# Thirteen products of the identity with itself on TensorE around the start of a decoder layer's output projection

## Chip, cores and metric

The kernel runs on one core of a Trainium2 chip. The metric is the device time of one execution in microseconds, here the median of three.

## What is computed

One pre-norm decoder layer over `x` (4 x 512 tokens, 512 wide): causal self-attention with 32 heads of width 16 in 8 key groups, cross-attention with 8 heads on `ctx_2048`, and a feed-forward part whose weights are rounded to -1, 0, 1 and whose activations are rounded to 8 bits.

```python
x = x + _L0_attn_ref(_layernorm(x), Wq, Wk, Wv, Wo)
x = x + _L0_xattn_ref(_layernorm(x), ctx_2048, ctx_2048)
x = x + _L0_ffn_ref(_layernorm(x), w_gate, w_up, w_down)

# in _L0_attn_ref
w = jax.nn.softmax(scores, axis=-1)
ctx = jnp.einsum('bgjqk,bkgd->bqgjd', w, v).reshape(b, s, D)
return ctx @ Wo.T
```

## The kernel before

The program has two blocks. Each gives every engine a list of instructions of its own; semaphores join them, and at a block's end all five engines meet (L237) before the next block begins.

**First block**, `attention`: `project_qkv` makes queries, keys and values batch by batch, and `self_attention` works in steps i. There are `COUNT` = 32 units (4 batches x 8 key groups, 4 heads each), and `LAST` = COUNT + 5 = 37, so i runs to 36. A step holds stages of several units: `first_scores` for unit i, `second_scores` for i - 2, `weigh` (probabilities by values, L870) for i - 3 and `turn_outputs` (L836) for i - 4. Each stage has its own test that the unit exists. In `turn_outputs` TensorE turns the unit's summed values (`b_osb`, copied out of PSUM by ScalarE at L797) with four transposes by the identity; VectorE then takes the reciprocal of the sums (L806) and writes the divided outputs into `tok` (L809), which holds all 16 token tiles.

**Second block**, `rest_of_layer`: `attend_output(c)` for c = 0, 1, ... works on 16 tiles of 128 tokens. On TensorE it turns tile c with four transposes (L1518), and then projects tile c - 1 with twelve matmuls of 128x512 (L1528): four slices of the contraction, each in three products of high and low parts (`hi`, `lo`, `wo_hi`, `wo_lo`). ScalarE writes the high part of the turned tile (L1211), VectorE the low part (L1354); TensorE waits for the low part ahead of the projection. VectorE then adds the rows of x (L1365, loaded by SyncE at L1023) and takes the moments (L1346, L1349), GpSimd makes the factor (L1150 to L1156), ScalarE normalises (L1217, L1222), VectorE splits (L1359), and SyncE stores the result to DRAM (L1028). SyncE's queue also carries the loads of context rows (L1010) and query rows (L1016) for the cross-attention. GpSimd begins the block with three memsets (L1129 to L1132). Cross-attention and the feed-forward part follow in `attend_context` and `feed`.

The order on each engine is that of the code. `ident` is a 128x128 identity in f32, `p2[0]` the PSUM bank `ab_j2` (in which second scores are made) and `pd` a bank that the second block first uses for the sums of cross-attention. At the kernel's start there is a function `rouse` already (L609): it multiplies ones by ones, f32 128x128, into a bank that nothing reads: 12 times at first, twice after the first batch's second tile is turned, and four times after its fourth.

Of the kernel before, what the change touches and what calls it, by code (L numbers as in the profile page):

```python
# [13 lines left out]
P = 128  # L14
# [37 lines left out]
def due(value):  # L52

    return not isinstance(value, int) or value > 0
# [21 lines left out]
class Steps:  # L76
# [3 lines left out]
    LAST = COUNT + 5  # L80
# [31 lines left out]
def bank_free(pe, st, keep, i, k):  # L112
    if st.holder(i, k) is not None:
        pe.wait_ge(keep["p1_used"], st.holder(i, k) + 1)


def first_scores(nc, pe, st, keep, i, k):

    if not i < st.COUNT:
        return  # L120
    s = i % UNROLL
    if k == 0:
        pe.wait_ge(keep["stacks_in"][s], 16 * st.STACK_LOADS * (i // UNROLL + 1))
    bank_free(pe, st, keep, i, k)
    for j, qt, c in st.units[k]:
        w = (qt + 1) * P
        last = nc.tensor.matmul(st.bank(keep, i, k)[:, c:c + w], keep["qs"][0:STACK, s, j, qt * P:(qt + 1) * P], keep["ks"][0:STACK, s, 0:w],  # L127
                                start=True, stop=True)
    last.then_inc(keep["p1_full"], 1)


def turn_maxima(nc, pe, st, keep, i):
    if 0 <= i - 1 < st.COUNT:
        pe.wait_ge(keep["p1_used"], st.use[i - 1, st.nu - 1] + 1)
        bank_free(pe, st, keep, i, st.TURN)
        nc.tensor.transpose(st.bank(keep, i, st.TURN)[0:st.BLOCKS, 0:P], keep["mx"][:, (i - 1) % 2, :], keep["ident"][:]).then_inc(keep["p1_full"], 1)
# [556 lines left out]
def self_attention(nc, ctx, io, scr, keep, st):  # L693


    STEPS, LAST = st.COUNT, st.LAST
# [11 lines left out]
    p2, pv = keep["p2"], keep["pv"]  # L708
# [16 lines left out]
    def pblock(s, kb):  # L725
        return probs[:, s, at[kb]:at[kb] + GSZ * width[kb]].rearrange("p (j w) -> p j w", j=GSZ)
# [97 lines left out]
    def tensor(pe):  # L824
        pe.wait_ge(keep["lo_done"], TILES)
        pe.wait_ge(keep["scaled"], 1)
        pe.wait_ge(keep["padded"], 2)
        for i in range(st.EARLY_STEPS, LAST):
            j2, j3, j4 = i - 2, i - 3, i - 4

            def turn_outputs():
                if 0 <= j4 < STEPS:
                    pe.wait_ge(osb_full, j4 + 1)
                    bank_free(pe, st, keep, i, OUT)
                    for t in range(TPB):
                        last = nc.tensor.transpose(st.bank(keep, i, OUT)[:, t * P:(t + 1) * P], osb[:, j4 % 2, t * P:(t + 1) * P], keep["ident"][:])  # L836
                    last.then_inc(p1_full, 1)

            def second_scores(n):

                if not 0 <= j2 < STEPS:
                    return
                kb, j0, nj, c, w = EXPS[n]
                s, unit = j2 % UNROLL, NE * j2 + n
                if n == 0:
                    pe.wait_ge(m_in[s], 32 * (j2 // UNROLL + 1))
                if due(unit - BANKS2 + 1):
                    pe.wait_ge(exps, unit - BANKS2 + 1)
                else:
                    pe.wait_ge(keep["rest_done"], BATCH * (DIM // P + 1) - BANKS2 + unit + 1)  # L850
                bank = p2[unit % BANKS2][:, 0:nj * w]
                last = nc.tensor.matmul(bank, ks[0:STACK + 2, s, kb * P:(kb + 1) * P],  # L852
                                        qs[0:STACK + 2, s, j0:j0 + nj, kb * P + c:kb * P + c + w], start=True, stop=c > 0)
                if c == 0:
                    last = nc.tensor.matmul(bank, keep["identb"][:], keep["mask_kq"][:].rearrange("p j c -> p (j c)"), start=False, stop=True)
                last.then_inc(scores, 1)

            def weigh(kb):

                if not 0 <= j3 < STEPS:  # L860
                    return
                if kb == 0:
                    if due(j3):
                        pe.wait_ge(osb_full, j3)
                    else:
                        pe.wait_ge(keep["v_kept"], BATCH)
                pe.wait_ge(exps, NE * j3 + EXPS_OF[kb])
                v = keep["v"][:, j3, kb, :]
                for j in range(GSZ):
                    last = nc.tensor.matmul(pv[2 * HDIM * j:2 * HDIM * (j + 1), kb * P:], v, pblock(j3 % 2, kb)[:, j, :],  # L870
                                            start=kb == 0, stop=kb == TPB - 1, skip_group_check=True)
                if kb == TPB - 1:
                    last.then_inc(weighted, 1)

            def F(k):
                first_scores(nc, pe, st, keep, i, k)

            S, W = second_scores, weigh
            F(0); S(0); F(1); S(1)
            turn_outputs()  # L880
            F(2); S(2)
            turn_maxima(nc, pe, st, keep, i)
            F(3); S(3)
            F(4); S(4)
            W(0); W(1); W(2); W(3)
            F(5); S(5); F(6); S(6); F(7); S(7); F(8); S(8); F(9); S(9); S(10)
# [4 lines left out]
def rest_of_layer(nc, io, scr, keep, out):  # L891
# [10 lines left out]
    with ExitStack() as ctx:  # L902
# [38 lines left out]
        p2 = [m.ps(f"p2{k}", [P, DIM]) for k in range(BANKS)]  # L941
# [570 lines left out]
        def _(pe):  # L1512
            def attend_output(i):
                if i < TILES:
                    if due(i - 1):
                        pe.wait_ge(C["lo"], i - 1)
                    for k in range(KD):
                        last = nc.tensor.transpose(tr[i % 2][:, k, :], tok[:, i, k * P:(k + 1) * P], keep["ident"][:])  # L1518
                    last.then_inc(C["turned"], 1)
                j = i - 1  # L1520
                if 0 <= j < TILES:
                    pe.wait_ge(C["lo"], j + 1)
                    if due(j - 1):
                        pe.wait_ge(C["x1"], j - 1)
                    n = 0
                    for k in range(KD):
                        for xp, wp in ((hi, "wo_hi"), (hi, "wo_lo"), (lo, "wo_hi")):
                            last = nc.tensor.matmul(pj[j % 2][:], xp[:, j % 2, k, :], keep[wp][:, k, :], start=n == 0,  # L1528
                                                    stop=n == 3 * KD - 1)
                            n += 1  # L1530
                    last.then_inc(C["projected"], 1)
# [85 lines left out]
            def feed(i):  # L1617
# [35 lines left out]
                if i - 4 != HELD:  # L1653
                    if i - 5 == HELD:
                        down(HELD)
                    down(i - 4)

            in_turn(attend_output, early, attend_context, feed, first=(25, 28))


# [70 lines left out]
```

## Time and profile before

| | us |
|---|---|
| median of three executions | 808.04 |
| the three | 808.04, 808.13, 806.4 |
| profiled execution, own time | 809.84 |
| profiled execution, span | 807.8 |
| TensorE busy with matmuls | 763.5 |
| VectorE busy | 642.9 |
| ScalarE busy | 480.2 |
| GpSimd busy | 424.3 |
| mean granted clock of TensorE | 0.989 |

The span runs from the first to the last instruction, and busy times are of the one profiled execution. A stretch is named by its microseconds from the span's start. The granted clock is 1.00 at 2.4 GHz and 0.50 at 1.2 GHz.

### The profile page before, as it was taken

To read this page: it belongs to the slowest core of one execution; us is meant where nothing else is said; L and a number is where in the kernel's file an instruction comes from. 1 tells how busy PE (TensorE), PEld (TensorE's weight loads), DVE (VectorE), ACT (ScalarE), POOL (GpSimd) and SP (SyncE) were. 2 spreads that over 40 slices of the span, in tenths; PEclk is the share of its full clock that TensorE was granted. 3 is DMA by queue.
4 is the path that set the end of the run, shared out by engine and by line. 5 is a ranking of instruction groups with operands and counts; after the bars stand their busy time and mean duration, and the time that the engine had idled before them with its cause. 6 is when DMAs were issued, how large, how long until landed. Compare 5 with 4: busy or idle time off the path is not lost.

```text
span 807.8 us, 14447 instructions
## 1 busy us (share of the span) xinstructions
PE 763.5 (95%) x4342; PEld 407.6 (50%) x4342; DVE 642.9 (80%) x1921; ACT 480.2 (59%) x844; POOL 424.3 (53%) x437
## 2 busy tenths in 40 slices
PE   8999999999979999998999699999899999999988
PEld 6777544444444444443877455554444344444433
DVE  7676888898878888881689778888975888888884
ACT  4666566676656776775455766666666455444452
POOL 5554479999994000001334577988878344432331
PEclk9999999999999999999999999999999999999999
DMA  8898664544431122101387655655552335333435
GB/s 291 302 377 289 205 194 129 156 129 152 155 104 51 51 66 62 51 26 29 123 277 244 190 158 162 172 169 163 163 157 62 54 77 105 75 84 78 86 79 130
DMA packets 112028, 113.61 MB, mean 141 GB/s; under 512 B 70640, under 2 KB 82160, under 8 KB 108880
## 3 DMA queue, kind: packets, MB, share of 16 engines
q1 hardware_dynamic: 109600, 99.66, 43.1%
q0 software_dynamic: 1840, 12.98, 4.7%
q8 instruction: 35, 0.57, 0.3%
q14 instruction: 41, 0.34, 0.1%
q10 hardware_dynamic: 512, 0.07, 0.1%
HBM read 81.26 MB, written 20.51 MB: 126 GB/s over the span
## 4 chain that ended last, share of the span: by engine, by line
PE 18%; DVE 15%; issue 6%; SPq 5%; POOL 4%; DMA 2%; ACT 2%; ACTq 0%; DVEq 0%; POOLq 0%
PE r_pn L1590 4%; DVE r_h L1431 3%; POOL r_h L1200 3%; PE r_p L1542 3%; PE r_p L1576 3%; PE r_p L1577 3%; PE r_pd L1600 1%; DVE r_hpart L1439 1%; PE r_p L1633 1%; DVE r_amax L1462 1%; PE r_pd L1650 1%; DVE r_zn L1460 1%; SPq L1016 1%; SPq L1010 1%; ACT r_silu L1307 1%
## 5 line engine op out<-in xcount | busy, mean ns | idle before, releaser
L787 ACT ACTIVATE b_probs<-ab_j 128x512 f32<-128x512 f32 (+1 forms) x352 | 176.6, 560 | 32.3 <-PE ab_j L852 13.5
L147 DVE CUSTOM_DVE_ANT_0 b_junk<-ab_t,mask_qk 128x128 bf16<-128x128 f32 (+2 forms) x243 | 108.8, 485 | 27.2 <-PE ab_t L127 26.9
L852 PE MATMUL ab_j<-qs,ks 98*128 98x512 bf16 (+1 forms) x352 | 122.4, 362 | 6.3 <-DMA qs<-mrow 5.2
L147 DVE CUSTOM_DVE_ANT_0 b_junk<-ab_e,mask_qk 128x256 bf16<-128x256 f32 (+2 forms) x237 | 104.1, 482 | 6.1 <-PE ab_e L127 5.6
L1268 ACT ACTIVATE r_probs<-r_p 128x512 f32<-128x512 f32 x128 | 74.0, 594 | 52.3 <-PE r_p L1577 51.0
L1376 DVE TENSOR_REDUCE r_mx<-r_p 128x1 f32<-128x512 f32 x128 | 86.4, 678 | 18.5 <-PE r_p L1542 17.3
L1167 POOL TENSOR_TENSOR r_halves<-r_probs 128x1024 f32<-128x1024 f32 x32 | 76.7, 2397 | 15.0 <-ACT r_probs L1268 13.0
L870 PE MATMUL ab_pv<-b_probs,v 128*32 128x512 f32 (+3 forms) x1024 | 75.5, 436 | 0.0
L1633 PE MATMUL r_p<-wg,r_zt 128*128 128x512 bf16 x256 | 65.8, 380 | 4.0 <-DMA r_zt<-r_zq 1.9
L1129 POOL MEMSET r_ql<- 64x2048 f32 x1 | 1.8, 1799 | 128.4 <-POOLq L237 128.4
L127 PE MATMUL ab_e<-ks,qs 96*128 96x128 bf16 (+3 forms) x269 | 64.1, 301 | 5.1 <-DMA ks<-k_parts 1.6
L1633 PE MATMUL r_p<-wu,r_zt 128*128 128x512 bf16 x256 | 65.8, 379 | 2.6 <-DVE r_h L1431 2.6
L1542 PE MATMUL r_p<-r_kk,r_qh 128*128 128x512 f32 x128 | 56.6, 443 | 8.4 <-DVE r_mx L1376 4.9
L1590 PE MATMUL r_pn<-r_probs,r_vt 128*64 128x512 f32 x256 | 61.1, 599 | 0.0
L127 PE MATMUL ab_t<-ks,qs 96*128 96x128 bf16 (+2 forms) x243 | 58.8, 303 | 2.2 <-DVE mx L147 0.2
L1200 POOL TENSOR_SCALAR r_h<-r_h,r_fh 128x1024 f32<-128x1024 f32 x32 | 36.6, 1155 | 37.6 <-DVE r_fh L1504 37.6
L1431 DVE TENSOR_TENSOR r_h<-r_p,r_silu 128x512 f32<-128x512 f32 x64 | 43.6, 681 | 13.9 <-ACT r_silu L1307 13.9
L870 PEld LDWEIGHTS ab_pv<-b_probs,v 128*32 128x32 f32 x1024 | 30.0, 109 | 48.3 <-issue 41.3
L797 ACT ACTIVATE b_osb<-ab_pv 128x512 f32<-128x512 f32 x32 | 19.1, 597 | 58.3 <-PE ab_pv L870 58.3
L1576 PE MATMUL r_p<-r_qh,r_kk 128*128 128x512 f32 x128 | 52.1, 407 | 1.7 <-DMA r_ql<-r_mrow 0.7
L1577 PE MATMUL r_p<-r_ql,r_kh 128*128 128x512 f32 x128 | 51.5, 402 | 0.0
L1307 ACT ACTIVATE r_silu<-r_p,r_cg 128x512 f32<-128x512 f32 x64 | 42.0, 678 | 14.9 <-PE r_p L1633 7.5
(167 smaller groups left out, 1668.1 us busy)
## 6 DMA issues: line engine op xcount, KB each, us to landing
r_k<-in_ctx SPq DMA_DIRECT2D x64, 128.0 KB, 2.7
r_qh<-x_normed_high SPq DMA_DIRECT2D x64, 128.0 KB, 2.7
qs<-q_parts SPq DMA_DIRECT2D x32, 192.0 KB, 3.2
q_parts<-a_parts SPq DMA_DIRECT2D x15, 384.0 KB, 6.0
a_wst<-in_w_gate SPq DMA_DIRECT2D x4, 1024.0 KB, 7.6
a_wst<-in_w_up SPq DMA_DIRECT2D x4, 1024.0 KB, 9.8
a_wst<-in_w_down SPq DMA_DIRECT2D x4, 1024.0 KB, 8.0
qs<-q_parts SPq DMA_DIRECT2D x32, 128.0 KB, 2.7
```

The costliest lines, as they stand in the source:

```text
L127: last = nc.tensor.matmul(st.bank(keep, i, k)[:, c:c + w], keep["qs"][0:STACK, s, j, qt * P:(qt + 1) * P], keep["ks"][0:STACK, s, 0:w], st ...
L147: best = nc.vector.tensor_tensor_reduce(out=junk[:, 2 * (st.use[i, k] % slots) + n, 0:w], in0=bank[:, c:c + w], in1=keep["mask_qk"][:, SEQ ...
L787: nc.scalar.activation(pblock(j % 2, kb)[:, j0:j0 + nj, c:c + w], p2[(NE * j + n) % BANKS2][:, 0:nj * w].rearrange("p (j c) -> p j c", j=n ...
L852: last = nc.tensor.matmul(bank, ks[0:STACK + 2, s, kb * P:(kb + 1) * P], qs[0:STACK + 2, s, j0:j0 + nj, kb * P + c:kb * P + c + w], start= ...
L870: last = nc.tensor.matmul(pv[2 * HDIM * j:2 * HDIM * (j + 1), kb * P:], v, pblock(j3 % 2, kb)[:, j, :], start=kb == 0, stop=kb == TPB - 1, ...
L1167: nc.gpsimd.tensor_tensor(halves[:], probs[:, j % PSLOTS, 0:2, :], probs[:, j % PSLOTS, 2:4, :], ALU.add).then_inc(halved, 1)
L1376: nc.vector.reduce_max(mx[:, (i - 1) % 2, n:n + 1], p1[use(i, k) % BANKS][:], AX.X).then_inc(p1_used, 1)
L1542: nc.tensor.matmul(p1[use(i, k) % BANKS][:], qh[:, j % QSLOTS, n * P:(n + 1) * P], kk[:, j % UNROLL, :], start=True, stop=True).then_inc(p ...
L1576: nc.tensor.matmul(bank[:], kk[:, j % UNROLL, blk], qh[:, j % QSLOTS, :], start=True, stop=False)
L1577: nc.tensor.matmul(bank[:], kh[:, j % 2, blk], ql[:, j % UNROLL, :], start=False, stop=True).then_inc(scores, 1)
L1590: last = nc.tensor.matmul(pn[a * H:(a + 1) * H, :], vt[:, j % UNROLL, nb, :], probs[:, j % PSLOTS, nb, :], start=nb == 0, stop=nb == KD - ...
L1633: last = nc.tensor.matmul(bank[g % BANKS][:], zt[:, j % 2, k, :], keep[w][:, k, n * 512:(n + 1) * 512], start=k == 0, stop=k == KD - 1)
```

## The change

`self_attention` gets a function `rouse` that multiplies the identity by itself into `p2[0]`, and a branch for the step LAST - 1 that calls it with 2 and with 5, with `turn_outputs` in between, and leaves the rest of the step out. `attend_output` gets six such products into `pd` where tile 0 is to be projected. No result of them is read.

```diff
@@ self_attention, tensor
             def F(k):
                 first_scores(nc, pe, st, keep, i, k)
 
+            def rouse(n):
+
+                for _ in range(n):
+                    nc.tensor.matmul(p2[0][:, 0:P], keep["ident"][:], keep["ident"][:], start=True, stop=True)
+
             S, W = second_scores, weigh
+            if i == LAST - 1:
+                rouse(2)
+                turn_outputs()
+                rouse(5)
+                continue
             F(0); S(0); F(1); S(1)
             turn_outputs()
@@ rest_of_layer, tensor, attend_output
                     last.then_inc(C["turned"], 1)
                 j = i - 1
+                if j == 0:
+                    for _ in range(6):
+                        nc.tensor.matmul(pd[:, 0:P], keep["ident"][:], keep["ident"][:], start=True, stop=True)
                 if 0 <= j < TILES:
                     pe.wait_ge(C["lo"], j + 1)
```

The instructions of the other engines stay in their order. On TensorE, at the end of the first block, the order before was (L836 are the last transposes of `turn_outputs`, L237 is the block's end):

```order
L870 MATMUL ab_pv<-b_probs,v 32x128 [waits b_exps]
L870 MATMUL ab_pv<-b_probs,v 32x128 x3
L836 MATMUL ab_e<-ident,b_osb 128x128 [waits p1_used,b_osb_full]
L836 MATMUL ab_e<-ident,b_osb 128x128 x3
L237 UNCONDITIONAL_BRANCH
L1511 UNCONDITIONAL_BRANCH [waits barrier_Pool_Activation_PE_DVE_SP_release]
```

and with the change it is (L881 is the product in the new `rouse`):

```order
L870 MATMUL ab_pv<-b_probs,v 32x128 [waits b_exps]
L870 MATMUL ab_pv<-b_probs,v 32x128 x3
L836 MATMUL ab_e<-ident,b_osb 128x128 [waits p1_used,b_osb_full]
L836 MATMUL ab_e<-ident,b_osb 128x128 x3
L881 MATMUL ab_j<-ident 128x128 x7
L237 UNCONDITIONAL_BRANCH
L1521 UNCONDITIONAL_BRANCH [waits barrier_Pool_Activation_PE_DVE_SP_release]
```

Two and five stand in one row of seven, behind the last four transposes and ahead of the meeting of the engines. Nothing stands between the last matmuls of `weigh` and the transposes.

On TensorE, at the start of the second block, the order before was (L1518 turns tiles 0 and 1, L1528 projects tile 0):

```order
L1518 MATMUL r_p<-ident,tok 128x128 x8
L1528 MATMUL r_p<-wo_hi,r_hi 128x512 [waits r_c_lo]
L1528 MATMUL r_p<-wo_lo,r_hi 128x512
L1528 MATMUL r_p<-wo_hi,r_lo 128x512
L1528 MATMUL r_p<-wo_hi,r_hi 128x512
```

and with the change, in which these lines are 1528 and 1541:

```order
L1528 MATMUL r_p<-ident,tok 128x128 x8
L1533 MATMUL r_pd<-ident 128x128 x6
L1541 MATMUL r_p<-wo_hi,r_hi 128x512 [waits r_c_lo]
L1541 MATMUL r_p<-wo_lo,r_hi 128x512
L1541 MATMUL r_p<-wo_hi,r_lo 128x512
```

The six stand behind the transposes of tile 1 and ahead of the wait for the low part of tile 0.

## Rows read from the trace of the kernel before

**Rows 1.** Page of before: busy time of the engines, granted clock in 40 slices
```profile
PE 763.5 (95%) x4342; PEld 407.6 (50%) x4342; DVE 642.9 (80%) x1921; ACT 480.2 (59%) x844; POOL 424.3 (53%) x437
...
PEclk9999999999999999999999999999999999999999
```

**Rows 2.** Windows around the block's end: length, busy (count) by engine, PEclk, DMA share, GB/s
```profile
378.00:379.00 1.00, 0.30 (x12) 0.03 (x4) 0.00 (x0) 0.60 (x1) 0.00 (x0) 1.00 0.00 0
...
380.00:381.00 1.00, 0.25 (x2) 0.28 (x3) 0.42 (x1) 0.00 (x0) 0.29 (x1) 0.95 0.00 0
...
382.00:383.00 1.00, 0.56 (x3) 0.16 (x1) 0.62 (x1) 0.74 (x2) 1.00 (x2) 0.50 0.84 270
...
385.00:386.00 1.00, 1.00 (x4) 0.81 (x3) 0.00 (x0) 0.00 (x0) 0.00 (x0) 0.50 0.11 41
```

**Rows 3.** Windows, two stretches of low clock
```profile
380.83:387.66 6.83, 6.27 (x19) 4.90 (x20) 1.38 (x2) 1.19 (x2) 3.52 (x3) 0.51 0.49 154
452.51:455.92 3.41, 3.41 (x10) 2.43 (x10) 2.63 (x5) 1.93 (x4) 3.03 (x2) 0.51 0.49 172
```

**Rows 4.** Timeline at the block's end: start, us, engine, line, operation, count, idle before
```profile
379.02 0.66 PE L836 MATMUL ab_e<-ident,b_osb 128*128 128x128 f32 x4 [0.72 <-ACT b_osb L797]
379.71 0.26 DVE L806 RECIPROCAL b_rec<-ab_e 128x16 f32<-128x16 f32 x1 [2.95 <-PE ab_e L836]
380.00 0.42 DVE L809 TENSOR_TENSOR tok<-ab_e,b_rec 128x256 f32<-128x256 f32 x1
380.71 1.80 SPq L1023 DMA_DIRECT2D r_x_in<-in_x  x4
...
380.75 1.81 PE L1518 MATMUL r_p<-ident,tok 128*128 128x128 f32 x8 [1.08 <-PEq L237]
381.75 0.60 ACT L1211 ACTIVATE r_hi<-r_p 128x512 fp32r<-128x512 f32 x1 [2.79 <-PE r_p L1518]
...
383.12 0.79 PE L1528 MATMUL r_p<-wo_hi,r_hi 128*128 128x512 f32 x1 [0.56 <-DVE r_lo L1354]
```

**Rows 5.** L237, the block's end: duration in ns (min/median/max), first and last start
```profile
L237 PEldq DRAIN  x1: 702/702/702, 379.0 to 379.0; - x1
L237 DVEq DRAIN  x1: 464/464/464, 380.0 to 380.0; - x1
```

**Rows 6.** Chain that ended last: start, us, what
```profile
383.12 5.14 PE r_p L1528 x12
...
406.77 3.35 DMA r_x_in<-in_x
```

**Rows 7.** Timeline of TensorE at the kernel's start
```profile
1.12 4.99 PE L609 MATMUL ab_j<-a_ones 128*128 128x128 f32 x24 [1.12 <-DVE a_ones L502]
...
7.62 0.66 PE L620 MATMUL ab_t<-ident,a_xn 128*128 128x128 f32 x4 [0.81 <-DVE a_xn L513]
8.12 0.61 PE L609 MATMUL ab_j<-a_ones 128*128 128x128 f32 x4
...
11.14 1.06 PE L609 MATMUL ab_j<-a_ones 128*128 128x128 f32 x8
...
26.32 1.04 PE L620 MATMUL ab_t<-ident,a_xn 128*128 128x128 f32 x8
27.11 0.48 PE L646 MATMUL ab_j<-a_xhi,a_whi 128*128 128x512 f32 x1
```

**Rows 8.** Timeline of GpSimd after the block's end
```profile
390.24 0.23 POOL L1150 TENSOR_SCALAR r_veps<-r_mv 128x1 f32<-128x1 f32 x1 [5.83 <-DVE r_mv L1349]
```

**Rows 9.** Timeline of TensorE, around the projections of tiles 1 and 2
```profile
388.11 0.60 PE L1518 MATMUL r_p<-ident,tok 128*128 128x128 f32 x4
...
391.66 0.48 PE L1528 MATMUL r_p<-wo_hi,r_hi 128*128 128x512 f32 x1
...
394.51 0.60 PE L1518 MATMUL r_p<-ident,tok 128*128 128x128 f32 x4
```

**Rows 10.** Window of a microsecond at the kernel's start
```profile
10.00:11.00 1.00, 0.35 (x3) 0.35 (x4) 0.95 (x2) 0.60 (x1) 0.01 (x1) 1.00 0.56 166
```

## The prediction

> **What bounds the kernel now.** I read the page first, then the granted clock, then the place of the change. By the page TensorE is busy 95% of the span, and its clock row shows no low slice [rows 1]; only one microsecond at a time does the dip show [rows 2]. The clock is full in the slice from 378, 0.95 in that from 380 and 0.50 in those from 382 and 385. It is one stretch of 6.83 us, from 380.83 to 387.66, at the lower of TensorE's two levels (1.2 instead of 2.4 GHz) [rows 3]. Ahead of it the engine was little occupied: busy 0.30 of the slice from 378 and 0.25 of that from 380 [rows 2].
>
> The timeline tells why it rests there [rows 4]. TensorE is idle 0.72 us, from 378.30, until ScalarE has copied the summed values, turns them in four transposes from 379.02 to 379.68, VectorE divides (0.26 and 0.42 us, done at 380.42), and then the block ends. Each engine has a DRAIN and then a meeting of all five [rows 5]: TensorE's DRAIN ends at 379.0 + 0.70 = 379.7, VectorE's, the last, at 380.0 + 0.464 = 380.46. SyncE begins the next block at 380.71 and TensorE at 380.75 [rows 4]. So **VectorE releases the next block, and TensorE has 0.76 us to spare** (380.46 less 379.70).
>
> In the next block TensorE turns token tile 0, ScalarE starts on it 1.00 us later, VectorE follows, and 1.37 us after ScalarE's start the first matmul of tile 0's output projection begins [rows 4]. In the chain that ended last its twelve matmuls take 5.14 us [rows 6], at the low clock. Here TensorE's pace sets the end.
>
> **Where the products land.** The step LAST - 1 is 36, and the outputs turned there would be those of head group 36 - 4 = 32; there are 32, numbered from 0. turn_outputs therefore issues nothing, and `rouse(2)` and `rouse(5)` are one row of seven behind the last four transposes and ahead of the block's end, as the order of the changed kernel shows. The first idle time, from 378.30 to 379.02, is not filled. The other six stand behind the transposes of tile 1, ahead of TensorE's wait for the low part of tile 0.
>
> **The price of one product.** The same product, f32 128x128 by 128x128, stands at the kernel's start with ones as operand. Twelve calls show as 24 passes, so a call is two. Two calls (x4) took 0.61 us and four calls (x8) 1.06 us [rows 7]: (1.06 - 0.61) / 4 = 0.1125 us a pass, over a constant tail. At the very start 24 passes took 4.99 us, 0.208 each [rows 7]; I take that for the low level.
>
> **Term 1: the block ends later.** The product row that follows four transposes started 0.50 us behind them (7.62 to 8.12) [rows 7], so the seven start at 379.02 + 0.50 = 379.52. Fourteen passes take 1.06 + 6 x 0.1125 = 1.74 us and end at 381.26. TensorE's DRAIN ended within 0.02 us of its last matmul [rows 4, 5]; at 381.27 it would be 0.81 us behind VectorE's and would release everybody. **+0.81 us.** Below, the bound is 0 (the DRAIN does not await them, or they fit in the 0.76 us), above, 14 x 0.208 + 0.2 = 3.1 us, ending at 382.6, which is +2.2. I take 0.81 since the nearest rows are of the same product at full clock. Queued behind are SyncE's four loads of x, GpSimd's memsets and the transposes. The loads keep the DMA engines busy to just past 385 (share 0.11 in the slice from 385 [rows 2]); 0.81 us later is 386, still ahead of the new end of tile 0's projection (386.8 below). GpSimd sat idle 5.83 us ahead of its first use [rows 8]. Both are covered; without that cover each would cost up to the 0.81 again.
>
> **Term 2: transposes at full clock.** From the first of four to the start of the engine that reads them it is 0.69 us at full clock (379.02 to 379.71) and 1.00 now (380.75 to 381.75) [rows 4]: **-0.31 us.** Between 0, if the clock is low, and -0.37 (they take 0.60 in a running stream, at 394.51 [rows 9], and 0.66 from idle).
>
> **Term 3: the six ahead of the projection.** Transposes start at 380.75 + 0.81 = 381.56. By data: 0.69 to ScalarE's start, then 1.37 to the matmul as now (381.75 to 383.12) [rows 4]: 383.62. By TensorE's queue: eight transposes issue in 0.79 us in a running stream (26.32 to 27.11) and 1.00 from idle (twice 0.50) [rows 7]; with 0.90 they are through at 382.46, and 12 x 0.1125 = 1.35 us of products lead to 383.81. The queue is later: **+0.19 us**, between 0.08 and 0.29.
>
> **Term 4: projection of tile 0 at full clock.** Now from its first matmul (383.12) to the transposes of tile 2 (388.11) is 4.99 us [rows 4, 9]; the same distance for tile 2 is 391.66 to 394.51, 2.85 us [rows 9]. **-2.14 us**, if the clock holds throughout; 0 if not at all.
>
> Sum: 0.81 - 0.31 + 0.19 - 2.14 = **-1.45 us.** The projection starts at 383.81 and ends (with its 0.2 of tail) at 386.8. What is late next? The chain goes on over tile 1 and the other engines to SyncE's queue, and at 406.77 to a load of x that takes 3.35 us [rows 6]. Each of these waits for something this block made, and nothing is bound to an absolute time, so I let the 1.45 pass whole; the bound is none of it.
>
> Of the 6.83 low microseconds these two terms return 2.45, less than half, because TensorE waited in part of the stretch (0.56 busy in the slice from 382 [rows 2]). The Trainium skill ("TensorE: Matmul & The Clock Gate", Terms) prices such a stretch as throttled time x (1 - K/N), an estimated 3.41 us here, with which the sum would be -2.41; the row on the waiting speaks against it.
>
> **Does the clock hold?** With the seven, TensorE is occupied from 379.02 to 381.26 and again from 381.56 without a gap to the end of tile 0, so its longest rest is the 0.72 us before 379.02. At the kernel's start the same mixture of four transposes and few products had rests as long, 0.81 us ahead of 7.62, and the slice from 10 was 0.35 busy at full clock [rows 7, 10]. I expect no fall here.
>
> **The rivals.**
> A, the block does not end later. The DRAIN does not await the seven, or they fit beside VectorE's work: 0.81 goes and the time is 808.04 - 2.26 = 805.8. Against it stands that both DRAINs I read end with their engine's last work. Chance 0.12.
> A2, the low stretch costs more. If in an ordinary execution TensorE works through all of the low stretch, half of its 6.83 us comes back, 3.41 instead of 2.45: 808.04 - 2.41 = 805.6. Against it stand the waits within it in this trace. Chance 0.10. This is also what the Trainium skill's formula, named above, gives.
> B, smaller gain. The low stretch is shorter, or lies elsewhere, in an execution without the profiler. Another in this trace lasted 3.41 us [rows 3]. Had this one ended 3.41 us earlier, only 1.1 us of the projection (383.12 to 384.24) would be low; that is 1.1 / 0.416 = 2.6 matmuls (4.99 / 12 each), and each saves 0.416 - 0.237 (2.85 / 12), 0.5 us in all instead of 2.14: the sum becomes 0.81 - 0.31 + 0.19 - 0.5 = +0.2. Times 806.9 to 808.3. For it speaks that the three times of before are 1.7 us apart. Chance 0.20.
> C, the clock seldom falls there without the change: only 0.81 and 0.19 remain, 809.0. Against it stands the trace. Chance 0.05.
> D, **slower.** The clock falls in spite of the products, since 378.30 to 379.02 stays empty. Then the six run low in front of the projection: transposes 1.7 us from 381.56 (1.81 for eight with tail [rows 4]), then 12 x 0.208 = 2.5, so it starts at 385.76 instead of 383.12, +2.64, which lands at 810.7 if the projection is as slow as now. It decides as soon as the clock is low when those six start. The start of the kernel speaks against it. Chance 0.10.
>
> **How the numbers follow.** The profiled execution's own time is 809.84 (span 807.8 and 2.0 around it), 1.8 above the median of 808.04. The sum makes it 808.39; against the median it is 808.04 - 1.45 = **806.6**. Chance of this case 0.43. A measurement of this kernel tells 0.2%, 1.62 us, from no change, and the forecast stands just inside. Of my case 0.17 lies beyond 1.62 and 0.26 within; A and A2 are faster (0.22); B is 0.19 within and 0.01 faster; C is within; D is 0.08 slower, 0.02 within. I move 0.02 from no change to slower for what I have not named: faster 0.40, same 0.50, slower 0.10. The range takes in A, A2, B and nearly C: 805.2 to 808.9.
>
> **What would show it.** Right: fourteen passes of about 0.11 us behind the last transposes; TensorE's DRAIN ends last, near 381.3; the next block starts near 381.5; twelve further passes behind tile 1's transposes; the first projection matmul near 383.8, waiting on no VectorE; the twelve in about 2.8 us; full clock from 378 to 390; the transposes of tile 2 near 386.7. Wrong: a next block at 380.7 (term 1 is nothing), a granted clock of 0.5 anywhere in the stretch (D), or a later wait, in SyncE's queue above all, that gives the 1.45 back.

## The result, and the profile after

The changed kernel took 810.13 us, the median of 22 runs (806.31 to 817.06), beside 807.29 us (804.74 to 810.23, 22 runs) for the kernel before on the same chip: a ratio of 1.0042 with a 95% interval of 1.0026 to 1.0058. By that ratio it is **slower by 3.4 us** (the two medians are 2.8 apart), where 1.45 less was forecast. The prediction was wrong in sign, and 810.1 lies above its range, 805.2 to 808.9. To "slower" it had given 0.10.

The profiled execution shows little of this: span 807.1 and own time 809.18, where before had 807.8 and 809.84. One execution of each is not the comparison; both kernels spread, over 5 and 11 us.

The page of the changed kernel, its TensorE row, answers to [rows 1]:

```profile
PE 764.0 (95%) x4368; PEld 407.5 (50%) x4368; DVE 647.0 (80%) x1921; ACT 480.2 (59%) x844; POOL 422.6 (52%) x437
```

Thirteen calls became 26 matmuls and 26 weight loads, 52 instructions more. The prediction did not use that number, and what follows turns on it.

The timeline of the changed kernel at the block's end (start, us, engine, line, operation, count, idle before) answers to [rows 4]:

```profile
375.15 0.66 PE L836 MATMUL ab_e<-ident,b_osb 128*128 128x128 f32 x4 [0.72 <-ACT b_osb L797]
...
375.65 1.73 PE L881 MATMUL ab_j<-ident 128*128 128x128 f32 x14
...
376.14 0.42 DVE L809 TENSOR_TENSOR tok<-ab_e,b_rec 128x256 f32<-128x256 f32 x1
377.63 1.80 SPq L1033 DMA_DIRECT2D r_x_in<-in_x  x4
...
377.67 1.06 PE L1528 MATMUL r_p<-ident,tok 128*128 128x128 f32 x8 [0.30 <-PEq L237]
378.34 1.08 ACT L1221 ACTIVATE r_hi<-r_p 128x512 fp32r<-128x512 f32 x2 [3.24 <-PE r_p L1528]
...
378.57 1.50 PE L1533 MATMUL r_pd<-ident 128*128 128x128 f32 x12
...
379.83 0.48 PE L1541 MATMUL r_p<-wo_hi,r_hi 128*128 128x512 f32 x1
...
382.69 0.60 PE L1528 MATMUL r_p<-ident,tok 128*128 128x128 f32 x4
```

And the two DRAINs of the block's end in the changed kernel (min/median/max ns, first and last start), which answer to [rows 5]:

```profile
L237 PEldq DRAIN  x1: 2170/2170/2170, 375.2 to 375.2; - x1
...
L237 DVEq DRAIN  x1: 461/461/461, 376.2 to 376.2; - x1
```

The whole program up to here ran 3.9 us earlier in this execution (transposes at 375.15, before 379.02), as the traces of one kernel differ among themselves (the kernel before, again: 376.18; in its first trace TensorE had stood 3.86 us for a load, `qs<-mrow`, until 237.53); so only distances within a stretch are compared. From the last transposes to SyncE's start of the next block it is now 377.63 - 375.15 = 2.48 us, before 1.69 [rows 4]: **+0.79**, forecast +0.81. TensorE's DRAIN ends at 375.2 + 2.17 = 377.4, 0.7 to 0.8 behind VectorE's. From SyncE's start to the transposes of tile 2 it is 382.69 - 377.63 = 5.06, before 388.11 - 380.71 = 7.40 [rows 4, 9]: **-2.34**, forecast -2.26. Each of the four terms landed as worked out: the later block end; then 0.67 us from the transposes to ScalarE (worked out 0.69), 2.16 from the transposes to the projection (2.25), and 2.86 for the projection (2.85). Here, the change does what it was costed to do.

Three windows of the changed kernel in the first six microseconds of that block (length, busy by engine, PEclk, DMA share, GB/s) answer to [rows 2]:

```profile
378.00:379.00 1.00, 1.00 (x11) 1.00 (x10) 0.03 (x1) 0.66 (x2) 1.00 (x1) 1.00 0.29 102
380.00:381.00 1.00, 1.00 (x6) 0.82 (x5) 0.25 (x1) 0.00 (x0) 0.94 (x2) 1.00 0.98 336
382.00:383.00 1.00, 1.00 (x7) 0.83 (x6) 0.12 (x1) 0.00 (x0) 0.00 (x0) 1.00 0.02 8
```

In these three TensorE is busy without a gap at full clock, where before had 0.50 in the last of them. So the loss lies elsewhere, and one place showed it: 400 us later, in the feed-forward, at the last turn of quantized activations (`r_zt<-r_zq`, a transposing load). The chain that ended last, before:

```profile
781.00 2.54 DMA r_zt<-r_zq
...
783.59 3.63 PE r_p L1633 x16
```

and in the changed kernel:

```profile
779.12 3.77 DMA r_zt<-r_zq
...
782.93 2.12 PE r_p L1646 x9
```

The same load of the same data takes 1.23 us longer, and TensorE waits for it: the timeline of before, then of the changed kernel, has

```profile
783.59 1.04 PE L1633 MATMUL r_p<-wg,r_zt 128*128 128x512 bf16 x4 [1.91 <-DMA r_zt<-r_zq]
```

```profile
782.93 1.04 PE L1646 MATMUL r_p<-wg,r_zt 128*128 128x512 bf16 x4 [3.13 <-DMA r_zt<-r_zq]
```

What else moved in that load's time? The DMA view of the changed kernel, over the load (busy tenths and GB/s in 40 slices of 0.095 us, where a packet counts with its whole time and size in the slice in which it starts; queues with packets, MB, share; issues with us to landing):

```profile
DMA  9999999999994699999997006960000007999988
GB/s 199 232 199 216 216 199 234 181 221 207 162 203 90 116 369 218 213 221 162 129 44 0 0 0 30 94 32 8 8 11 11 11 8 224 388 453 496 388 345 345
...
q8 instruction: 1, 0.02, 1.4%
...
out<-r_res SPq DMA_DIRECT2D x1, 256.0 KB, 3.1
r_zt<-r_zq SPq DMA_TRANSPOSE x1, 3.8
```

and that of before, over its own, which is shorter (slices of 0.065 us):

```profile
DMA  9999999999999999854589999998542000019599
GB/s 217 213 221 205 213 201 228 185 221 217 197 224 189 232 169 205 158 99 91 91 177 221 197 224 197 228 205 193 114 84 44 8 0 0 0 32 284 158 410 441
...
out<-r_res SPq DMA_DIRECT2D x1, 256.0 KB, 2.3
r_zt<-r_zq SPq DMA_TRANSPOSE x1, 2.5
```

In the changed kernel one packet of the queue "q8 instruction" falls into the load. It starts 1.4 us behind the load's start and takes 0.88 us. Near the load's end only 8 to 11 GB/s start in each of six slices in a row, hardly a sixteenth of the some 200 at its beginning. It looks as if one of the sixteen engines, held up by the packet, still has its part to move and everybody waits for it; that is a reading of these rates, since the trace does not name the engine of a packet. Before, that packet passes 3.7 us after the load's start, when the load is over. The page gives this queue 35 packets and 0.57 MB over the run, 16 KB each; a second queue of that name, q14, has 41 smaller ones. The Trainium skill ("Trainium Architecture — The Big Picture", The software stack) says that an instruction is 64 bytes; by that TensorE's 8,736 come to 0.559 MB, an estimate, which fits the queue, with some 256 instructions to a packet. That section speaks of the streams only as moved to the engines when the program is loaded; here 35 packets move during the run.

That gave a theory, called I below: **the 52 instructions move TensorE's instruction fetches against the rest of the program**, and one of them now meets a small load that TensorE waits for. The rivals: the later end of the block costs it; the six do; the higher clock upsets SyncE's queue; the chip differs.

### The profile page after: what moved, and what is told of

The parts are those of the page before. It is cut to its first block, busy times and chain, and to the rows that moved or that the text cites. A ratio compares the mean times of both kernels' runs of the same rounds, so it can differ in the third digit from the quotient of the medians.

```text
span 807.1 us, 14499 instructions
## 1 busy us (share of the span) xinstructions
PE 764.0 (95%) x4368; PEld 407.5 (50%) x4368; DVE 647.0 (80%) x1921; ACT 480.2 (59%) x844; POOL 422.6 (52%) x437
## 4 chain that ended last, share of the span: by engine, by line
PE 23%; DVE 12%; issue 6%; SPq 4%; POOL 4%; DMA 3%; ACT 2%; DVEq 0%; ACTq 0%; POOLq 0%
PE r_pn L1603 5%; PE r_p L1646 4%; PE r_p L1589 3%; PE r_p L1555 3%; POOL r_h L1210 3%; DVE r_h L1441 3%; PE r_p L1590 3%; PE r_pd L1613 2%; DMA r_x_in<-in_x 1%; PE r_pd L1663 1%; DVE r_hpart L1449 1%; SPq L1020 1%; DVE r_amax L1472 1%; DVE r_stats L1356 1%; DMA r_ql<-r_mrow 1%
```

## The experiments

In every table below, times are medians, the ratio is to the kernel before on the same chip, in the same round.

**The two kernels again, and each half of the change.** The first of these is the kernel before, unchanged.

> The kernel before once more, for its second trace and for the granted clock of each execution. Theory L (the 6.83 us low stretch at the block's end is usual): low clock again between 378 and 390, and executions with a lower mean clock take longer, about half of the added low time. Theory S (that stretch was chance in the first trace): it is absent or 3.4 us here. Ratio to the kernel before 1.000 +- 0.001 by both.

> The changed kernel once more. It measured 810.13 against 807.29, where my sum said 1.45 less. Theory F (the clock falls in spite of the products in part of the executions, and then the six run low ahead of the projection): mean clocks between 0.983 and 0.994, the longest executions with the lowest; ratio again about 1.004. Theory E (the low time is elsewhere, after the output projection): this trace too shows full clock around 375 to 385 and more low time around 440 to 460 or 580 to 600 than the kernel before.

One half drops the six of the projection, the other the seven of the block's end:

```diff
 seven_only, against the changed kernel
-                if j == 0:
-                    for _ in range(6):
-                        nc.tensor.matmul(pd[:, 0:P], keep["ident"][:], keep["ident"][:], start=True, stop=True)
 six_only, against the changed kernel
-            if i == LAST - 1:
-                rouse(2)
-                turn_outputs()
-                rouse(5)
-                continue
```

> Only the seven products ahead of the block's end; the six in front of the projection are gone. Theory F: the seven alone cost the 0.8 us of the later block end and bring most of the gain where the clock holds, so 806.5 to 808 (ratio 0.999 to 1.001). If the six are what costs, this is clearly faster than the changed kernel, by 2 us or more. Theory E: as slow as the changed kernel (ratio 1.003 to 1.004), since the later stretches do not depend on the six.

> Only the six products in front of the projection. The clock falls at the block's end as before, so they run low: 12 x 0.208 = 2.5 us, and transposes of 1.7 us, so the first matmul of the projection starts 380.75 + 1.7 + 2.5 = 384.95 instead of 383.12, +1.8 us (ratio 1.002), less where more of the projection then falls behind the clock's return. Theory F: 1.002 to 1.003. Theory E: 1.000 to 1.002, below the changed kernel.

| kernel | runs | us | ratio | 95% |
|---|---|---|---|---|
| before (reference) | 34 | 807.75 | | |
| before_again | 12 | 807.14 | 0.9998 | 0.9977 to 1.0018 |
| after_again | 11 | 811.47 | 1.0036 | 1.0015 to 1.0056 |
| seven_only | 12 | 808.85 | 1.0015 | 0.9996 to 1.0034 |
| six_only | 12 | 807.78 | 1.0006 | 0.9985 to 1.0027 |

The loss repeats on another chip, and neither half has it whole. A sum of halves would allow 0.0015 + 0.0006, so the point estimates are short of 0.0036, though the intervals do not exclude it. The traces say more. In before_again the clock did not fall at the block's end at all (windows: us, busy by engine, PEclk):

```profile
378.00:380.00 2.00, 1.02 (x9) 0.79 (x9) 0.79 (x2) 1.09 (x2) 2.00 (x2) 1.00 0.53 125
380.00:382.00 2.00, 2.00 (x9) 1.65 (x10) 0.50 (x1) 0.00 (x0) 1.51 (x2) 1.00 0.90 296
```

Here TensorE rested exactly as in [rows 4], 0.72 and 1.08 us, and its clock stayed full; of the expectations' theories, S holds and L does not. F is not seen either: neither trace of the changed kernel has a low clock at the block's end, nor has the third one below. E is not borne out: low stretches between 430 and 610 us add up to 10.2 us in both traces of the changed kernel so far and to 6.8 in both of the kernel before, but also to 10.2 in both halves, seven_only and six_only. In six_only the seven are missing and the clock did fall, for a shorter time, and on the six themselves (TensorE's timeline):

```profile
377.83 1.40 PE L1523 MATMUL r_p<-ident,tok 128*128 128x128 f32 x8 [1.08 <-PEq L237]
379.03 2.76 PE L1528 MATMUL r_pd<-ident 128*128 128x128 f32 x12
381.44 0.66 PE L1536 MATMUL r_p<-wo_hi,r_hi 128*128 128x512 f32 x1
```

The twelve passes take 2.76 us instead of 1.50 and hold the projection up. This is what rival D feared for the changed kernel; in these traces it takes the seven away to get it. And both halves, 28 and 24 instructions longer, wait 1.80 and 1.85 us for the last `r_zt`, like before.

**The instruction count alone, and other ways to issue the same products.** pad_52 is the kernel before with 26 one-column products strewn over self-attention, 52 instructions with no product at the change's place:

```diff
+                if n == 0 and 5 <= i < 31:
+                    nc.tensor.matmul(bank[:, 0:1], keep["identb"][:], keep["identb"][:, 0:1], start=True, stop=True)
```

> The kernel before with 26 tiny bf16 products (one column, about 0.05 us) spread over 26 steps of self-attention, each overwritten at once: as the change, it puts 52 TensorE instructions (26 weight loads, 26 matmuls) ahead of all that follows, with nothing at the block's end. Theory I (the added instructions shift where TensorE's 16 KB instruction blocks are fetched, and one fetch meets the last transposing load of r_zt): the stretch from result 11 to result 15 is 24.7 us instead of 23.4, a fetch lies in that load, and the kernel is 1.2 to 2.5 us slower than before (ratio 1.0015 to 1.003). Theory P (the products at the block's end cost it all): 23.4 us there, ratio 1.000 to 1.0005.

realigned is the changed kernel with the 18 products of the kernel's start issued as 5 wide ones, 52 instructions fewer, so that all behind is numbered as before:

```diff
-            for _ in range(n):
-                nc.tensor.matmul(pj[0][:, 0:P], ones[:], ones[:], start=True, stop=True)
+            for at in range(0, n, 4):
+                w = min(4, n - at)
+                nc.tensor.matmul(pj[0][:, 0:w * P].rearrange("p (j c) -> p j c", j=w), ones[:],
+                                 ones[:].unsqueeze(1).broadcast_to([P, w, P]), start=True, stop=True)
```

> The changed kernel, but the 18 products of ones at the kernel's start are written as 5 wide ones with the same columns, which takes 52 TensorE instructions away: the second block is where it was before the change. Theory I: 23.4 us from result 11 to 15, block end still 0.8 us later, six still 0.1, so 0 to 0.9 us slower than before (1.000 to 1.001) and 2 us or more faster than the changed kernel. Theory P: ratio 1.0036 as the changed kernel.

wide issues the change's own thirteen as four wide products of up to 512 columns (16 instructions more). fitted puts five, as two wide ones, in the two idle times at the block's end, which its step LAST - 2 reaches, and has no six (8 instructions more). In both `rouse` issues up to four products as one call; its text is left out here:

```diff
 wide
+            if i == LAST - 1:
+                turn_outputs()
+                rouse(7)
+                continue
...
+                    for w in (4, 2):
 fitted
+            if i == LAST - 2:
+                rouse(3)
+                turn_outputs()
+                rouse(2)
+                continue
```

> The changed kernel with its 13 products written as 4 wide ones of the same columns: TensorE is occupied as long (about 1.5 and 1.3 us) with 16 instructions instead of 52. Theory I: block end 0.8 us later, no fetch in the last r_zt load, 23.4 us from result 11 to 15, ratio 1.000 to 1.0012. Theory P: ratio 1.0036.

> Products where they cost nothing by the profile: one of three columns' worth (3 x 128) in the idle 0.72 us ahead of the last four transposes (step LAST - 2), one of 2 x 128 behind them, inside the 0.76 us that TensorE has to spare, none in front of the projection; 8 instructions more than before. By theory I and by the terms of my sum the block ends as before (1.69 us from the last transposes to the next block), the clock seldom falls, and only the gain is left: 0 to 1.5 us faster than before, ratio 0.998 to 1.000. Theory P with any product costing more than its time: above 1.001.

| kernel | runs | us | ratio | 95% |
|---|---|---|---|---|
| before (reference) | 35 | 808.81 | | |
| pad_52 | 12 | 811.40 | 1.0049 | 1.0024 to 1.0074 |
| realigned | 12 | 810.72 | 1.0038 | 1.0014 to 1.0062 |
| wide | 12 | 807.87 | 0.9992 | 0.9971 to 1.0014 |
| fitted | 12 | 807.46 | 0.9995 | 0.9968 to 1.0022 |

pad_52 has none of the change's products and costs as much as the change, and more than the 1.003 that was expected. The time of its own 26 products does not show where they stand: its last transposes of the block begin at 376.07, those of before_again at 376.18. Its wait for the last `r_zt` is 3.30 us, and its load is met by the packet too (DMA view over the load):

```profile
q8 instruction: 1, 0.02, 1.4%
...
out<-r_res SPq DMA_DIRECT2D x1, 256.0 KB, 3.3
r_zt<-r_zq SPq DMA_TRANSPOSE x1, 3.9
```

wide does all the change's work with 16 instructions, ends the block as late (2.42 us), and costs nothing that can be measured. So neither the later end of the block, nor the columns of the six, nor the clock that is kept is what costs. fitted fills the rests (TensorE's timeline; the first row now stands where 0.72 us were idle):

```profile
374.46 0.91 PE L882 MATMUL ab_j<-ident 128*128 128x384 f32 x2
375.25 0.66 PE L836 MATMUL ab_e<-ident,b_osb 128*128 128x128 f32 x4
375.74 0.60 PE L882 MATMUL ab_j<-ident 128*128 128x256 f32 x2
376.98 1.06 PE L1530 MATMUL r_p<-ident,tok 128*128 128x128 f32 x8 [0.64 <-PEq L237]
```

It keeps the clock, ends the block no later than before (1.69), and still gains nothing that can be measured. realigned spoke against the theory: its wait is 1.86 us, the late load is gone, but the time is still lost; at most 1.001 had been expected. So either the theory was wrong or the merged start costs something by itself. The next group has that control.

**The control, and the 52 at two other places.** merged_start is the kernel before with realigned's edit alone. pad_ffn has the 26 one-column products ahead of the first 13 banks each of gate and up, behind attention; pad_out has two for each tile from 3 on in the output projection:

```diff
 pad_ffn
+                        if g < 13:
+                            nc.tensor.matmul(bank[g % BANKS][:, 0:1], keep["identb"][:], keep["identb"][:, 0:1], start=True, stop=True)
 pad_out
+                    for _ in range(2 if j >= 3 else 0):
+                        nc.tensor.matmul(pj[j % 2][:, 0:1], keep["identb"][:], keep["identb"][:, 0:1], start=True, stop=True)
```

> The kernel before with the 18 products of ones at its start written as 5 wide ones (52 instructions fewer, shift by -52 for all that follows). It is the control for realigned, which measured 1.0038 where theory I said at most 1.001. If the start alone costs something (another clock, self-attention's fetches at other places), this kernel is at 1.002 to 1.003 as well, with a late first block; if it is at 1.000, realigned's loss belongs to its seven and six products and theory I explains only the tail.

> The kernel before with the same 26 tiny bf16 products, now in the feed-forward part only (first 13 gate and up banks of tiles 0 to 3, overwritten at once). The instructions are shifted by 52 only behind them, so only fetches from tile 4 on move. Theory I: the fetch meets the last r_zt load (24.7 us from result 11 to 15, +1.3), nothing else changes: ratio 1.001 to 1.0025. If the tail stays at 23.4 the shift is not the cause of it.

> The same 26 tiny products in the output projection of tiles 3 to 15 (two each, overwritten at once). Cross-attention and feed-forward are shifted by 52 instructions, self-attention is untouched. Theory I: +1.3 in the tail and what fetches in cross-attention cost (147 to 148 us from output 0 to output 13 instead of 145 to 146), together 1.002 to 1.005, near pad_52. If it stands at pad_ffn's value, cross-attention does not mind the shift and the rest of pad_52's loss lies in the first block.

> The fitted version once more, for its difference to the kernel before: by the terms 0 to 1.5 us faster (0.998 to 1.000); first result 0.9995 with 807.46 against 808.81 by medians. The block again ends 1.69 us after the last transposes, tail 23.4 us.

| kernel | runs | us | ratio | 95% |
|---|---|---|---|---|
| before (reference) | 35 | 808.28 | | |
| merged_start | 12 | 810.52 | 1.0039 | 1.0012 to 1.0065 |
| pad_ffn | 12 | 808.80 | 1.0011 | 0.9988 to 1.0035 |
| pad_out | 12 | 809.95 | 1.0022 | 0.9999 to 1.0046 |
| fitted_again | 12 | 807.10 | 0.9995 | 0.9974 to 1.0015 |

merged_start costs 1.0039 by itself. So realigned (1.0038) has lost what that control loses, and nothing beyond it: it no longer speaks against the theory. The loss lies in the first block, whose last transposes begin at 379.58 us in merged_start and at 379.21 in realigned; in twelve of the fourteen other traces they begin at 375.15 to 377.39, and the two later ones, before and seven_only, stood 3.86 and 3.44 us for a load of `mrow`. In merged_start TensorE waits long for a load of keys (timeline), and the clock falls behind that:

```profile
114.11 0.42 PE L127 MATMUL ab_e<-ks,qs 96*128 96x128 bf16 x2 [3.56 <-DMA ks<-k_parts]
```

The DMA view of the tenth of a microsecond in which that load is issued, from 104.8, gives its time to landing:

```profile
ks<-k_parts SPq DMA_DIRECT2D x1, 16.0 KB, 9.2
```

A packet of q8 starts at 109.84, within these 9.2 us, and one of q14 0.4 us behind it. In realigned the load takes 8.3 us, a packet of q8 starts in it at 110.47, and TensorE waits 2.66 us. In the fourteen other traces the packet has passed by then, at 97.6 to 99.8, no load of keys or queries there takes over 7.5 us, and TensorE waits at most 1.64. So the merged start seems to lose its time in the theory's own way, at another load. These are two traces and nothing was varied to test it: likely, not shown. They also tell whose packets these are: with 52 TensorE instructions fewer at the kernel's start the first packet of q8 starts at 30.9 us in both, and at 22.8 to 23.7 in the fourteen others.

pad_ffn and pad_out both have the late load, 3.09 and 3.34 us of wait, with the 52 added far behind those of pad_52. Their times, 1.0011 and 1.0022, lie between the kernel before and the changed kernel, with intervals that reach no change. So where the 52 stand matters too, or the rest is chance; the runs do not tell which. The expectation for pad_out had a place for it, fetches in cross-attention; the section on the prediction comes back to that. Both traces show what the late load can bring. The windows of pad_out behind it:

```profile
784.00:787.00 3.00, 1.36 (x4) 0.54 (x5) 2.83 (x7) 1.72 (x2) 0.00 (x0) 0.61 0.62 153
787.00:790.00 3.00, 3.00 (x9) 1.07 (x8) 1.20 (x5) 0.69 (x1) 2.22 (x2) 0.50 0.83 196
```

TensorE stood 3.34 us, its clock fell, and for the next 6.8 us the matmuls run at 1.2 GHz, with TensorE the bound (3.00 of 3.00 busy).

**More instructions instead of fewer.** If the count's place in the fetches decides, adding another 52 to the changed kernel should help it. after_plus_26 is the changed kernel with pad_ffn's edit; after_third is the changed kernel once more, in the same rounds.

> The changed kernel, all its 13 products kept, with 26 tiny products more in the feed-forward part (as in pad_ffn), so that the shift ahead of the tail is 104 instructions instead of 52. Theory I: the fetch that met the last r_zt load comes earlier, ahead of that load; TensorE waits 1.8 to 2.0 us for it instead of 3.1 to 3.3, the clock does not fall in the tail, and the kernel is 1 to 3 us faster than the changed kernel although it issues more (ratio about 1.001 to 1.002). If the wait stays above 3 us, more instructions ahead of the tail are bad in themselves and it is not the place of the fetch.

> The changed kernel on the same chip, for the comparison with after_plus_26: ratio 1.003 to 1.005, a wait of 3.1 to 3.3 us for the last r_zt load, and a low stretch behind that wait in part of the executions (the two traces so far had none there, pad_ffn and pad_out had 3.4 and 6.8 us).

| kernel | runs | us | ratio | 95% |
|---|---|---|---|---|
| before (reference) | 23 | 807.34 | | |
| after_plus_26 | 12 | 808.04 (806.55 to 809.44) | 0.9997 | 0.9975 to 1.0019 |
| after_third | 12 | 810.88 (808.60 to 818.42) | 1.0049 | 1.0024 to 1.0073 |

It does. All thirteen products are in, 26 more are added, and the loss is gone: 2.84 us faster than the changed kernel beside it, between medians, and the intervals of the two ratios do not meet. In its trace the load is back at its old length (the chain that ended last):

```profile
780.68 2.47 DMA r_zt<-r_zq
...
783.20 2.98 PE r_p L1648 x13
```

while after_third shows the low clock of pad_out, 3.4 us of it, in its last stage (windows; PEclk 0.51 in the middle row):

```profile
783.40:784.40 1.00, 0.99 (x5) 0.51 (x6) 0.93 (x3) 0.12 (x1) 0.00 (x0) 0.96 0.58 112
784.40:787.80 3.40, 3.40 (x10) 1.21 (x8) 2.25 (x8) 0.69 (x1) 2.22 (x2) 0.51 0.86 199
787.80:790.00 2.20, 2.20 (x12) 0.98 (x10) 1.14 (x2) 1.07 (x2) 0.00 (x0) 1.00 0.00 0
```

**All sixteen traces side by side**, by the place of the instruction packet against the start of the last `r_zt` load (to the microsecond), the load's landing time from the chain, TensorE's wait for it, and the tail (from VectorE's sum for result tile 11, `r_res`, to that for tile 15, numbered from 0), in us:

| traces | instructions added | packet | landing | wait | tail |
|---|---|---|---|---|---|
| before, before_again | 0 | 3 to 4 behind | 2.54, 2.56 | 1.91, 1.92 | 23.43, 23.45 |
| fitted, fitted_again, wide, six_only, seven_only | 8, 8, 16, 24, 28 | 3 to 5 behind | 2.44 to 2.60 | 1.80 to 1.96 | 23.32 to 23.49 |
| realigned | 0 | 3 to 4 behind | 2.49 | 1.86 | 23.39 |
| merged_start | -52 | none within 10 | 2.59 | 1.95 | 23.48 |
| after_plus_26 | 104 | 10 to 11 ahead | 2.47 | 1.83 | 23.36 |
| after, after_again, pad_52 | 52 | 1 to 2 behind | 3.77, 3.97, 3.95 | 3.13, 3.33, 3.30 | 24.66, 24.86, 24.83 |
| pad_ffn, pad_out, after_third | 52 | 1 to 2 behind | 3.74, 3.98, 3.94 | 3.09, 3.34, 3.29 | 26.21, 27.73, 26.50 |

There is nothing between the two kinds: ten loads land in 2.44 to 2.60 us, and the six that the packet meets in 3.74 to 3.98. The last three of the six have a fallen clock behind the wait besides. That 28 instructions or fewer leave the packet where it was, and 52 do not, is what the traces show; from which number on it moves was not tried.

## Why the prediction was wrong, point by point

**Right.** All seven products in one row behind the last transposes; the price of a pass (fourteen took 1.73 us, worked out 1.74); term 1 (+0.79, forecast +0.81), with TensorE's DRAIN as the last; terms 2 to 4 together (-2.34, forecast -2.26), where the clock would have fallen; the projection waiting on no VectorE. The 0.208 us for a pass at the low clock was taken from a row for which the view gives full clock (window 1 to 6 us: 1.00), but twelve passes at the low clock took 2.76 us in six_only, which bears it out. The clock never fell at the block's end in any of the nine traces with products ahead of it. A is refuted. D did not happen in any of the nine: its low clock on the six is there only without the seven. That its 810.7 lies near the measured 810.1 is luck.

**The failed step, 1: the cost of a product.** "Fourteen passes take 1.06 + 6 x 0.1125" counts a product as time on TensorE alone, and puts at nothing what its instructions do elsewhere. A call is also four instructions, and thirteen calls move everything behind them by 52 places in a stream that is fetched in 16 KB packets while the data moves. In this kernel that makes a load land 1.2 to 1.5 us later, 400 us on, on the path: +1.4 us of tail (24.78, the mean of the three without a fallen clock, less 23.41, that of the ten). In three traces of six the clock falls behind it, for another 1.4, 3.0 and 1.7 us, some 1.0 on average.

**The failed step, 2: the end of the sum.** "... nothing is bound to an absolute time, so I let the 1.45 pass whole; the bound is none of it." The sentence bounds the effect of the later stages at zero and never considers a loss. It did not hold: this change renumbers every later instruction of TensorE, and its largest single effect that the traces show, the late load, came 400 us behind the stage in which it stands.

**The failed step, 3: one trace taken as the rule.** "Against it stands the trace" (of C). Seven traces have no product ahead of the block's end. In four the clock falls there: 6.8 us in before, pad_ffn and pad_out, 3.4 in six_only. In three it does not: before_again, pad_52, merged_start. There the changed kernel gains nothing and pays its 0.79 and 0.10 (5.06 less the 4.96 of before_again). The fall costs 2.44 us (7.40 less 4.96) where it lasts 6.8 us, in three of the seven, and less in six_only. So on average terms 2 and 4 are worth 3/7 to 4/7 of 2.44, an estimate of 1.0 to 1.4 us, against 0.9 of cost: **the change's own gain is about half a microsecond at most**, which no measurement here could tell from none. Rival C, to which 0.05 was given, is thus three traces of seven; the average falls into the range of B. fitted holds the clock without delaying the block, so by this estimate it should gain 1.0 to 1.4 us, a ratio of 0.9983 to 0.9987. It gave 0.9995, twice, and both intervals hold that as well as nothing: the gain is not shown.

The Trainium skill ("TensorE: Matmul & The Clock Gate", Terms) prices a low stretch at its length times (1 - K/N), an estimated 3.41 us for this one; 2.44 us on the path was measured, since TensorE waited in part of it.

**The sum put right.** 0.9 of cost, less 1.0 to 1.4 of gain, plus 1.4 for the late load and 1.0 for the clock behind it, gives +1.9 to +2.3 us, where 3.4 [2.1 to 4.7] was measured, 2.9 and 4.0 in the repeats. Shown are the sign, and that the loss comes with the number of instructions and not with the products: pad_52 has the loss without the products, and after_plus_26 the products without the loss. The late load is the part of it that the traces show; that the packet makes it late rests on all sixteen traces and on two changes of the count, 52 and 104. **Not settled** is the remaining 1 to 2 us. The low stretches behind the wait may be more frequent than in six traces; for that speak the long executions, at or above 814 us in 8 of 45 of the changed kernel and 2 of 149 of the kernel before. In the 22 runs of the first comparison time falls as the granted clock rises (correlation -0.75), but in the 11 of the second it does not (-0.01). The mean clock of the changed kernel was 0.990, 0.992 and 0.990; that of the kernel before, recorded beside the last two, 0.991 and 0.992. Or the loss lies in cross-attention: from tile 2's transposes to the first matmul of the feed-forward the six traces with 52 instructions ahead of or in that stretch took 238.4 to 239.9 us, 239.2 on average, and the ten others 235.3 to 238.7, 237.4 on average; the low stretches between 430 and 610 us add up to 11.4 and 8.5 us. That is of the size that is missing. But after_plus_26 is one of the six (239.5) and lost nothing in total, so this stays a lead.

## What to carry to other kernels

Count an added product in instructions, too: the four kernels with 52 more of them were 0.1 to 0.5% slower (the 0.1 and 0.2% are not clear of nothing), though little of that is the products' own time, and wide products held the clock as well with 16. When a change leaves its own stage as forecast and the total goes the other way, add the same number of harmless instructions without the change, and double them with it. And take a second trace before costing a stretch of low clock: in this kernel it is there in four traces of seven.

## What the runs showed of the hardware

35 packets of 16 KB on the queue "q8 instruction" move during the run, and they go with TensorE's instructions: with 52 of these fewer at the start the first comes at 30.9 us and not at 22.8 to 23.7. When one falls into a 2.5 us transposing load, the load takes 3.7 to 4.0 us, as six traces show and none of the other ten; in the changed kernel only 8 to 11 GB/s start in a stretch near its end. The 256 KB store behind it took 3.1 to 3.3 us in place of 2.3, in all six.

TensorE's clock fell in one execution and not in another behind the same rests of 0.72 and 1.08 us. The stretches at 1.2 GHz were 3.4 or 6.8 us long, at the block's end and behind the late load alike.
